# An attention and feed-forward layer in five in-order queues: block diagonals by ScalarE, new statistics for the input norm, new orders

## The reference

```
h   = norm(x)
a   = softmax(causal(h Wq (h Wk)^T / sqrt(512))) h Wv + h          # one head, 32x32 within an entry
h1  = LN(a);  c = softmax(h1 Wcq (ctx Wck)^T / sqrt(512)) ctx Wcv + h1
h2  = LN(c);  x1 = x + relu(LN(relu(h2 W1 + b1) + h2))
x2  = x1 + (softmax(causal(16 heads of norm(x1) W_attn)) * decay) V W_proj
out = x2 + LN(silu(n sw1 + sb1) * (n sw2 + sb2)) sw3 + sb3         # n = norm(x2)
```

## Time and profile before

| | us |
|---|---|
| median of 3 runs | 1451.22 (1449.34 to 1452.15) |
| profiled execution, span from the first to the last instruction | 1452.8 |
| PE busy | 1365.6 |
| VectorE busy | 1128.1 |
| ScalarE busy | 601.9 |
| GpSimd busy | 526.1 |

### The profile page before, as it was taken

How to read it: one execution, slowest core, us unless ns; L and a number is a source line. 1 busy time by engine, 2 the same in 40 slices (tenths; PEclk the granted TensorE clock), 3 DMA queues, 4 the chain that set the end, 5 groups by cost and what they waited for, 6 DMA issues and landing times.

```text
span 1452.8 us, 33270 instructions
## 1 busy us (share of the span) xinstructions
PE 1365.6 (94%) x13860; PEld 851.7 (59%) x13861; DVE 1128.1 (78%) x2335; ACT 601.9 (41%) x1147; POOL 526.1 (36%) x545
## 2 busy tenths in 40 slices
PE   7679999999999999999999999999999999998888
PEld 3355566666656666665665656666665666655443
DVE  6787777777787877778778877777778877777776
ACT  2544444443444444343434444444444444443222
POOL 0133333433444333443443333343443433343222
PEclk9899999999999999999999999999999999999899
DMA  9732444433333444433333344443333344434440
GB/s 349 259 131 74 146 146 146 144 123 105 133 112 115 146 146 146 146 137 101 122 130 105 139 146 146 146 142 114 111 138 105 123 146 146 147 134 161 149 161 30
DMA packets 38662, 201.41 MB, mean 139 GB/s; under 512 B 5096, under 2 KB 5992, under 8 KB 28400
## 3 DMA queue, kind: packets, MB, share of 16 engines
q1 hardware_dynamic: 37648, 198.93, 38.3%
q10 hardware_dynamic: 864, 0.36, 0.1%
HBM read 182.24 MB, written 17.04 MB: 137 GB/s over the span
## 4 chain that ended last, share of the span: by engine, by line
PE 70%; DVE 19%; POOL 4%; ACT 4%; issue 3%; DMA 0%; DVEq 0%; POOLq 0%; ACTq 0%; SPq 0%
PE ps_a L1716 11%; PE ps_a L1739 8%; PE ps_t L1739 7%; PE ps_t L1703 6%; PE ps_a L1725 6%; PE ps_a L1751 4%; PE ps_a L1783 4%; POOL rstd L636 4%; PE ps_t L1716 3%; PE ps_v L1716 3%; DVE stats L1178 3%; DVE arena L1309 3%; PE ps_t L1826 2%; PE ps_t L1775 2%; PE ps_t L1751 2%
## 5 line engine op out<-in xcount | busy, mean ns | idle before, releaser
L645 POOL TENSOR_TENSOR act_l<-act_t,act_h 128x512 f16<-128x512 f32 (+1 forms) x176 | 199.5, 1134 | 351.4 <-ACT act_t L789 199.4
L636 POOL TENSOR_TENSOR rstd<-var,mhalf 128x1 f32<-128x1 f32 x224 | 181.8, 812 | 333.7 <-DVE var L1180 328.9
L781 ACT ACTIVATE act_h<-ps_t,scale 128x512 f16<-128x512 f32 (+1 forms) x110 | 70.8, 644 | 206.2 <-PE ps_t L1703 206.2
L645 POOL TENSOR_TENSOR last_slot<-last_slot 128x512 f16<-128x512 f32 x80 | 90.0, 1125 | 156.7 <-ACT last_slot L789 90.8
L1739 PE MATMUL ps_a<-act_h,arena 128*128 128x128 f16 x1408 | 87.6, 221 | 17.3 <-ACT act_h L781 17.3
L1739 PEld LDWEIGHTS ps_a<-act_h,arena 128*128 128x128 f16 x1408 | 81.9, 99 | 28.3 <-ACT act_h L781 21.3
L789 ACT ACTIVATE act_t<-ps_t,scale 128x512 f32<-128x512 f32 (+1 forms) x110 | 70.3, 639 | 49.1 <-PE ps_t L1703 49.1
L1739 PE MATMUL ps_t<-act_h,arena 128*128 128x128 f16 x1408 | 87.0, 221 | 3.3 <-ACT act_h L781 3.3
L1716 PE MATMUL ps_a<-arena,act_h 128*128 128x512 f16 x352 | 83.6, 380 | 1.9 <-ACT act_h L781 1.9
L1309 DVE TENSOR_SCALAR arena<-ps_a,unscale 32x512 f32<-32x512 f32 x64 | 48.2, 753 | 47.0 <-PE ps_a L1751 45.8
L1739 PEld LDWEIGHTS ps_t<-act_h,arena 128*128 128x128 f16 x1408 | 81.4, 99 | 4.9 <-DVE arena L1037 2.4
(11 more groups left out here) (380 smaller groups left out, 3150.7 us busy)
## 6 DMA issues: line engine op xcount, KB each, us to landing
arena<-in_ctx_t SPq DMA_DIRECT2D x32, 2056.0 KB, 8.4
arena<-in_ctx_n SPq DMA_DIRECT2D x32, 2048.0 KB
ctx_last<-in_ctx_last SPq DMA_DIRECT2D x32, 256.0 KB
arena<-in_ew SPq DMA_DIRECT2D x8, 1024.0 KB, 6.3
x_in<-in_x SPq DMA_DIRECT2D x22, 256.0 KB, 7.3
x_scratch<-rows SPq DMA_DIRECT2D x22, 256.0 KB, 8.8
out<-rows SPq DMA_DIRECT2D x22, 256.0 KB, 2.1
arena<-in_ew SPq DMA_DIRECT2D x8, 512.0 KB, 7.2
```

The lines of the kernel that those rows point to most:

```text
L636: nc.gpsimd.tensor_tensor(rstd[s][:], var[s][:], mhalf[:], ALU.pow).then_inc(rstd_ready[s], 1)
L645: nc.gpsimd.tensor_tensor(act_l[s][:, chunks], act_t[s][:, chunks], act_h[s][:, chunks], ALU.subtract).then_inc(act_l_ready[s], 1)
L781: nc.scalar.activation(act_h[s][:, 0:width // P].rearrange("p c r -> p (c r)"), bank[s][:, 0:width], ACT.Copy, scale=scale[:, k:k + 1]).th ...
```

## The change

Heads 2 and 3 of kbd are evacuated by ScalarE too (project_k2). The weights of the heads are transposed in place by one VectorE instruction and copied into pbd by ScalarE in four (heads_p, heads_p2); both arrays change their layout, so that a block is written as one run and read as four. The self-attention weights are transposed by VectorE instead of PE and ScalarE. The input norm gets buffers for its statistics and semaphores of its own, so that it can run before its slot's last tile is done. The bias of the last product is added to x2 by GpSimd (x2_bias) instead of in ffn_out. The scale of the scores is folded into earlier factors, so the maximum is negated in the reduction itself. The last instruction of a chain no longer holds the VectorE queue; the unit that reads its result waits for it. PE's project_self waits for ffn_out of the slot's last tile. All tables are new; of them ORDER for PE and VectorE and the beginning of LAST for PE are shown.

```diff
 ORDER = {
-    "pe": [(2, "project_q"), (3, "turn_z"), (2, "project_k_l"), (3, "ffn_out"), (3, "ffn_out_l"), (1, "turn_pc"),
-        (2, "project_q_l"), (1, "context_mix"), (2, "head_scores"), (0, "turn_xn"), (2, "project_v"),
-        (0, "project_self"), (0, "project_self_l"), (1, "turn_w"), (2, "project_v_l"), (1, "context_out"),
-        (0, "self_scores"), (1, "context_out_l"), (0, "value_self"), (0, "value_self_l"), (0, "turn_p"),
-        (2, "head_mix"), (0, "self_mix"), (2, "project_out"), (1, "turn_h2"), (2, "project_out_l"), (1, "hidden"),
-        (1, "hidden_l"), (0, "turn_h"), (2, "turn_x2n"), (0, "project_query"), (0, "project_query_l"), (2, "ffn_in"),
-        (0, "context_scores"), (2, "ffn_in_l"), (1, "turn_x1n"), (1, "project_k")],
-    "dve": [(3, "z_norm"), (2, "project_k"), (3, "ffn_out"), (0, "xn_moments"), (1, "context_total"), (0, "turn_xn"),
-        (2, "head_scores"), (1, "context_mix"), (1, "context_scaled"), (2, "head_total"), (0, "project_self"),
-        (2, "head_weights"), (0, "self_scores"), (1, "context_out"), (1, "context_norm"), (0, "self_mix"),
-        (2, "project_out"), (0, "self_norm"), (2, "x2_norm"), (1, "hidden"), (1, "out_norm"), (1, "x1_norm"),
-        (2, "ffn_in"), (0, "context_scores"), (2, "silu")],
...
+    "pe": [(1, "project_self_l"), (3, "project_v_l"), (2, "context_out"), (2, "context_out_l"), (1, "value_self"),
+        (1, "self_scores"), (1, "value_self_l"), (3, "head_mix"), (2, "turn_h2"), (1, "self_mix"),
+        (3, "project_out"), (3, "project_out_l"), (2, "hidden"), (1, "turn_h"), (2, "hidden_l"),
+        (1, "project_query"), (1, "project_query_l"), (3, "turn_x2n"), (1, "context_scores"), (3, "ffn_in"),
+        (2, "turn_x1n"), (3, "ffn_in_l"), (1, "turn_pc"), (2, "project_k"), (1, "context_mix"),
+        (2, "project_k_l"), (3, "turn_z"), (2, "project_q"), (2, "project_q_l"), (3, "ffn_out"),
+        (3, "ffn_out_l"), (0, "turn_xn"), (2, "head_scores"), (2, "project_v"), (1, "turn_w"),
+        (0, "project_self")],
+    "dve": [(4, "ffn_out"), (2, "context_scaled"), (3, "head_scores"), (3, "head_total"), (3, "head_weights"),
+        (1, "project_self"), (2, "context_out"), (1, "self_scores"), (2, "context_norm"), (1, "turn_p"),
+        (1, "self_mix"), (1, "self_norm"), (3, "project_out"), (2, "hidden"), (3, "x2_norm"), (2, "out_norm"),
+        (2, "x1_norm"), (1, "context_scores"), (0, "xn_moments"), (3, "ffn_in"), (0, "turn_xn"), (3, "silu"),
+        (3, "z_norm"), (1, "context_total"), (1, "context_mix")],
...
 }
 LAST = {
-    "pe": [(2, "project_q"), (3, "e_in4"), (3, "turn_z"), (2, "project_k_l"), (3, "ffn_out"), (3, "ffn_out_l"),
-        (1, "turn_pc"), (2, "project_q_l"), (2, "e_zt1"), (1, "context_mix"), (2, "head_scores"), (2, "e_in3"),
-        (0, "turn_xn"), (2, "project_v"), (2, "project_v_l"), (1, "turn_w"), (2, "e_out1"), (0, "project_self"),
-        (1, "e_turn"), (0, "project_self_l"), (1, "e_logits"), (0, "value_self"), (1, "e_in0"), (0, "self_scores"),
-        (2, "e_zt2"), (1, "context_out"), (1, "context_out_l"), (0, "value_self_l"), (0, "turn_p"), (2, "head_mix"),
...
+    "pe": [(4, "e_in2"), (3, "turn_h2"), (2, "self_mix"), (4, "head_mix"), (3, "hidden"), (3, "e_turn"),
+        (3, "hidden_l"), (4, "e_out0"), (4, "project_out"), (2, "turn_h"), (4, "project_out_l"),
+        (3, "e_logits"), (3, "e_in0"), (4, "e_zt1"), (2, "project_query"), (4, "e_in3"), (2, "project_query_l"),
+        (4, "turn_x2n"), (2, "context_scores"), (4, "ffn_in"), (3, "turn_x1n"), (4, "ffn_in_l"), (4, "e_out1"),
+        (4, "e_zt2"), (4, "e_out2"), (2, "turn_pc"), (3, "project_k"), (3, "project_k_l"), (3, "project_q"),
+        (4, "turn_z"), (2, "context_mix"), (3, "project_q_l"), (4, "ffn_out"), (4, "ffn_out_l"), (4, "e_zt3"),
...
 }
...
-            kbd = of_arena(HALF + 5 * C * D + 16, C * G * HPC * T).rearrange("p (c g h k) -> p c g h k", c=C, g=G, h=HPC)
-            pbd = of_arena(HALF + 6 * C * D + 16, NH * G * T).rearrange("p (h g q) -> p h g q", h=NH, g=G)
+            kbd = of_arena(HALF + 5 * C * D + 16, C * G * HPC * T).rearrange("p (h c g k) -> p h c g k", c=C, g=G, h=HPC)
+            pbd = of_arena(HALF + 6 * C * D + 16, NH * G * T).rearrange("p (g h q) -> p g h q", h=NH, g=G)
...
+                def x2_bias(s, r, tile):
+                    pool.wait_ge(rows_ready[s], 5 * r + 4)
+                    pool.wait_ge(x2_stored[s], 16 * r + 32)
+                    if tile == 0:
+                        pool.wait_ge(late_loaded, 16 * 7)
+                    nc.gpsimd.tensor_tensor(rows3[s][:], rows3[s][:], b3[:], ALU.add).then_inc(x2_biased, 1)
...
-                    nc.scalar.activation(p_n[s][:, 0:P], rows3[s][:, 0:P], ACT.Exp, bias=ntop[s][:], scale=XSCALE,
+                    nc.scalar.activation(p_n[s][:, 0:P], rows3[s][:, 0:P], ACT.Exp, bias=ntop[s][:],
                                          accum_out=total[s][:, 0:1]).then_inc(p_ready[s], 1)
-
-                def turn_p(s, r, tile):
-                    act.wait_ge(p_turned[s], 2 * r + 1)
-                    nc.scalar.copy(p_t[s][:, 0:P], ps_a[s][:, 0:P]).then_inc(p_t_ready[s], 1)
...
-                    for h in (0, 1):
-                        rows = slice(HD * h, HD * (h + 1))
-                        nc.scalar.activation(kbd[rows, :, :, h, :],
-                                             ps_a[s][rows, :].rearrange("p (c g k) -> p c g k", c=C, g=G), ACT.Copy,
-                                             scale=unscale[rows, K_WATTN:K_WATTN + 1]).then_inc(k_ready[s], 1)
...
+                def key_blocks(heads):
+                    def unit(s, r, tile):
...
+                        for h in heads:
+                            mine = slice(HD * h, HD * (h + 1))
+                            nc.scalar.activation(kbd[mine, h, :, :, :].rearrange("p c g k -> p (c g k)"),
+                                                 ps_a[s][mine, :], ACT.Copy,
+                                                 scale=unscale[mine, K_WATTN:K_WATTN + 1]).then_inc(k_ready, 1)
+                    return unit
+
+                def weight_blocks(groups):
+                    def unit(s, r, tile):
+                        act.wait_ge(heads_turned, tile + 1)
...
+                        for g in groups:
+                            mine = slice(T * g, T * (g + 1))
+                            nc.scalar.copy(pbd[mine, g, :, :].rearrange("p h q -> p (h q)"), rows3[s][mine, :]
+                                           ).then_inc(pbd_ready, 1)
+                    return unit
...
+                def made_by(name, s, r):
+                    dve.wait_ge(dve_step[s], steps_in_all * r + steps_before[name] + STEPS[name])
...
+                        self.last(ins)
+                        dve.wait_ge(dve_step[self.s], steps_in_all * self.r + steps_before[self.unit] + self.count)
+
+                    def last(self, ins):
                         self.count += 1
                         assert self.count <= STEPS[self.unit]
                         ins.then_inc(dve_step[self.s], 1)
...
-                    moments(chain, s, x_in[s][:], 1e-5)
-                    chain.end()
+                    nc.vector.bn_stats(x_stats[s][:], x_in[s][:]).then_inc(x_step, 1)
+                    dve.wait_ge(x_step, 2 * tile + 1)
+                    nc.vector.bn_aggr(x_mv[s][:], x_stats[s][:]).then_inc(x_step, 1)
+                    dve.wait_ge(x_step, 2 * tile + 2)
+                    nc.vector.tensor_scalar(x_var[s][:], x_mv[s][:, 1:2], 1e-5, None, ALU.add).then_inc(x_var_ready, 1)
 
                 def xn(s, r, tile):
-                    plain_norm(s, r, 1, rows1[s][:], x_in[s][:]).then_inc(rows_ready[s], 1)
+                    dve.wait_ge(x_rstd_ready, tile + 1)
+                    if tile >= SLOTN:
+                        dve.wait_ge(turned[s], 7 * r - 1)
+                    nc.vector.tensor_scalar(rows1[s][:], x_in[s][:], x_mv[s][:, 0:1], x_rstd[s][:], ALU.subtract,
+                                            ALU.mult).then_inc(x_rows, 1)
 
...
-                    chain(nc.vector.reduce_max(top[s][:, 0:1], rows3[s][:, 0:P], AX.X))
-                    nc.vector.tensor_scalar(ntop[s][:], top[s][:, 0:1], -XSCALE, None, ALU.mult
-                                            ).then_inc(ntop_ready[s], 1)
+                    nc.vector.reduce_max(ntop[s][:], rows3[s][:, 0:P], AX.X, negate=True).then_inc(ntop_ready[s], 1)
+                    chain.end()
+
+                def turn_p(s, r, tile):
+                    chain = Chain("turn_p", s, r)
+                    dve.wait_ge(p_ready[s], 3 * r + 1)
+                    nc.vector.transpose(p_t[s][:, 0:P], p_n[s][:, 0:P]).then_inc(p_t_ready[s], 1)
+                    chain.last(nc.vector.reciprocal(inv[s][:, 0:1], total[s][:, 0:1]))
                     chain.end()
...
-                    dve.wait_ge(decayed[s], r + 1)
-                    if tile == 0:
-                        dve.wait_ge(consts_ready, 5)
-                    else:
```

(25 more changed lines are left out.)

275 lines of the change are left out of this document (140 added, 135 removed), and 11 rows, old and new, of the table FIRST.

## The result

The changed kernel takes 1501.0 us (median of 4, 1499.2 to 1502.7), the kernel before 1451.7 beside it (4 runs, 1449.3 to 1452.3): a ratio of 1.035, 95% interval 1.033 to 1.036. It is slower by 49 us where I forecast 25 us faster, and outside my range. The profiled execution has a span of 1500.9.

What follows compares the result with a forecast made beforehand. PE, busy 94%, was taken as the bound. Middle rounds -10.9 (26 at -0.42), last order -6.4 and -3, first order -5 gave -25.3: span 1452.8 to 1427.5, predicted median 1426 us, range 1403 to 1447.

Steps and rivals of the forecast that it cites:

- the one on GpSimd beside VectorE: Shared port pair: an added GpSimd pass can hold a two-input VectorE instruction up to 1.2; VectorE idle then in the walk.
- turn_p, -0.20: Middle round: the self-attention weight transpose leaves PE for VectorE, saving 0.20 us of PE work a round.
- project_k, -0.95: Middle round: fillers ahead of project_k cover ScalarE's evacuation, so PE's 0.95 us wait goes, provided ScalarE is free.
- turn_x2n: Middle round: x2_norm now stands behind hidden on VectorE, so PE waits 1.28 us instead of 0.55, +0.73.
- Other units ... arrive within some 0.1: Middle round: turn_h2, self_mix, turn_z, ffn_out, head_scores arrive within 0.1 of PE's need or earlier; uncertainty +-0.3 a round.
- the small waits that I had left alone: Middle round: some 0.5 us of PE waits spread over GpSimd's remainders, taken as unchanged.
- x2_bias at nothing: GpSimd's bias addition waits for x2's store, 8.8 us from issue; judged just in time, cost zero.
- Strided blocks at nothing: PE reads kbd and pbd in four runs of 32 words; taken as zero, at worst +1.08 each for head_mix and head_scores.
- The last order, -6.4 and -3: Last order: two full rounds fall from 43.61 to 40.4, -6.4; expert's first turn moves a round later, -3.
- The first order, -5: First order: -0.42 in four rounds plus relief from VectorE's set-up pieces; not walked, bounds -12 to +8, taken as -5.
- B, collisions: Rival: ScalarE copies or late GpSimd keep a middle round about 40.6, only edges gain; 1441 (1438 to 1448), chance 0.20.
- D, the clock: Rival: the concentrated wait at turn_x2n makes PE's clock fall in every middle round; slower, 1465 to 1504, chance 0.08.

Runs made afterwards that it cites:

- experiment 1: GpSimd's remainder passes past a slot's first tile cut to one element per partition: changed kernel 1433.8 us, kernel before with the same cut 1443.4 us.
- experiment 2: Changed kernel with only one remainder pass per tile, that of turn_h, cut to one element per partition: 1469.7 us.
- experiment 4: Changed kernel with turn_h2's pass ahead of self_mix on GpSimd: 1484.8 us; with also turn_h behind hidden_l on PE: 1455.8 us.
- experiment 6: Changed kernel's instructions with the middle-round orders of the kernel before, first and last rounds as in the changed kernel: 1491.2 us.
- Experiment 3: Changed kernel with x2_norm put back ahead of hidden in VectorE's list of a middle round: 1570.5 us.

## Why the prediction was wrong

**The step that failed** is the one on GpSimd beside VectorE, "by it an added pass on GpSimd can hold a two-input VectorE instruction up to its own 1.2. In my walk VectorE is idle then." I priced the rule for the one added pass, at nothing, and left out the eight passes a tile that were there before. What the runs showed in its place: six VectorE instructions of a round are held for 5.2 us, four of them are ones that PE waits for, and a middle round takes 42.42 where I had 40.22. Without the passes it takes 40.22 (experiment 1). The passes had cost next to nothing in the kernel before because its order started each of them while VectorE was in an instruction that isn't held, or just behind the begin of one that is (13.4 us in all, experiment 1). The pass of 628.70 above is one of the latter. The new order takes this away, and my walk carried VectorE's durations over from the earlier trace rows as if they belonged to the instructions. They belong to the order too.

**Term by term**, for a middle round:
- turn_p, -0.20: right; it is gone from PE.
- project_k, -0.95: right; no wait is left there.
- turn_x2n: I had 1.28 lost where 0.55 was; it is 1.91. The pattern was right (VectorE ends the wait, hidden then x2_norm), the size off by the hold on the relu-and-add, 0.92, of which 0.3 is covered by PE's own wait ahead of project_query_l. With that pass gone (experiment 2) 1.31 is lost here, nothing at project_query_l, and the round fell by 0.92.
- "Other units ... arrive within some 0.1": wrong. turn_h 0.56, turn_x1n 0.53, turn_z 0.43 and project_query_l 0.33, together 1.85. The first three stand behind held instructions. The last stands behind turn_h's own pass, and 0.32 is lost there where self_norm isn't held too (experiment 4, GpSimd's exchange alone). Without the passes all four are gone.
- Sum: -0.20 - 0.95 + 1.36 + 1.85 = +2.06, less 0.28 of the small waits that I had left alone (0.35 before, 0.07 now), against +1.78 measured (42.42 - 40.64).
- x2_bias at nothing: right for this order; the store is the price I named, and where the cover is gone (experiment 6) it costs 33 us.
- Strided blocks at nothing: right; head_mix keeps 1.08, head_scores goes from 1.06 to 1.08. VectorE's transpose of the self-attention weights takes 0.30, as I had estimated.
- The last order, -6.4 and -3: net -3.4. The rounds gained less than I said: from tile 28 to tile 30 they take 41.07 and 41.23 for 41.93 and 43.61, 3.2 less. The lag falls by 16.3 up to tile 31 (51.5 to 35.2), but 13.1 of this is expert work that in the kernel before stands ahead of tile 31's context_out (1347.02 to 1360.10, with the wait of 2.77 and the product of 6.71) and now comes behind it. There the product takes 3.68 at full clock, as I had hoped, and a new wait of 3.90 with a fall of the clock behind it spends that gain: 12.9 are given back by the end. In the kernel after:

```profile
1403.01 0.66 PE L1731 MATMUL ps_t<-ident,rows 128*128 128x128 f32 x4 [3.90 <-DVE rows L1232]
...
1404.69 3.45 PE L1750 MATMUL ps_a<-arena,act_h 128*128 128x512 f16 x8
...
1412.68 3.68 PE L1905 MATMUL ps_a<-arena,last_slot 128*128 128x512 f32 x8
```

- The first order, -5: +1.4, namely 5.1 late at tile 0 and 3.7 won back by tile 3. I didn't walk it, and no run here takes it apart; that stays open.
- In all, forecast and result lie 73 us apart (-25.3 and +48.1 by the spans): 61 in the middle, 12 at the edges. So the holds are the main error, but the edges alone put the forecast 12 too low.

**The rivals.** B, collisions, named "GpSimd late" and priced the round at 40.6: it has the two engines in each other's way, but by lateness and not by a hold, and far too small. D, the clock, had the right place and the right sign, and six falls came where I said that from about 10 on the kernel is slower. It explains 6 of 49 us; that its 1465 to 1504 held the result is luck. Experiment 3 shows D almost whole: a wait of 2.9 in each middle round, and a fall behind 25 of the 26.

**The order and not the edits.** With an order that avoids most holds, the changed instructions take 1434.8. In the old order they bring nothing: 1457.9 with the bias on VectorE, and 33 us more with x2_bias. Whether the instructions of before could gain as much from a new order wasn't run; in the walk the same exchanging of neighbours brings them from 40.70 to 40.56 only.
